# First attention layer of an audio tower: scores over 32-row tiles, in two parts around the transposes of x_q

## The chip, the cores and the metric

The kernel runs on one core of a Trainium2 chip. The metric is the device time of one execution in microseconds (us). Before the change three executions took 4547.76, 4551.70 and 4551.86 us, a median of 4551.7 us. The core has a matrix engine (TensorE, PE in the profile, with its weight loads listed apart as PEld), a vector engine (DVE), a scalar engine (ACT), a general engine (POOL) and a queue for transfers (SP). Each runs its own list of instructions strictly in the order in which it was written, and they meet only at semaphores.

## The reference

The input is 64 sequences of 375 frames of 256 features. What is computed is this; the change touches the fourth line alone.

```
x  = conv(x, width 2, stride 2) + mean of the two frames      # 64 x 188 x 256
h  = layernorm(x) * gamma + beta
q, k, v = layernorm(h) @ qkv_proj.T + qkv_bias                # 16 heads of 16
attn = softmax(SCALE * einsum('bld,bmd->blm', q, k))          # b: token and head; l, m: the 64 sequences
h  = h + einsum('blm,bmd->bld', attn, v) @ out_proj.T + out_bias
xq = fp4_quant_dequant(layernorm(h))                          # blocks of 16
h  = h + fp4_quant_dequant(silu(xq @ wgate) * (xq @ wup)) @ wdown
h  = h + linear_attention(layernorm(h))                       # second layer, 16 heads of 64
h  = h + 0.5 * ffn(layernorm(h))                              # second layer
```

The attention of the first layer goes over the first axis of its input, so for each of the 188 tokens and each of the 16 heads there is a 64 x 64 table of scores with an inner size of 16.

## The kernel before, in words

`layer0` handles two tokens at a time: a tile has 128 rows, 64 sequences of one token and 64 of the next, and there are 94 tiles (`TILES`). The work is a software pipeline written out by hand. Each engine has a function `slot(t, par)`, and slot `t` holds the convolution of tile `t`, the attention of tile `t-1` and `t-2`, and the feed-forward part of the tiles `t-3` and `t-4`. Slots 0 to 5 and the last ones are written out; the ones between are a loop over pairs of slots. `exists(t, lag)` leaves out what has no tile. The order of the calls in each `slot` is the order on that engine, and nothing else decides it. `bank_free` and `wait` are waits on counts of finished steps.

On TensorE the slot runs: `conv`, `v_product` (L340), `xq_transpose` (L331, tile `xq`), `scores` (L369), then `gate(t, 0)`, `att_transpose`, `hq_transpose`, `up(t, 0)`, `outproj`, `gate(t, 1)`, `up(t, 1)`, `down`, `ln1_transpose`, `p_transpose`, `qk_product` and `pv_product` (L464). The products written as `product3` (L1093 to L1095) are three matmuls over high and low parts. A plain fp32 matmul shows as two weight loads and two matmuls in the records.

The scores need one block per head. Heads have 16 features, and a matmul takes 64 rows (4 heads) at a time. So `k_copy` on ACT (L571) writes k four times into `kblk`, each copy with all heads but one of each four masked to zero by the per-row scale `rowmask` and the masked bias `kb_masked`:

```python
for j in range(4):
    act.activation(kblk[:, c, :, j, :], src, ACT.Identity, bias=kb_masked[:, c, j:j + 1],
                   scale=rowmask[:, j:j + 1]).then_inc(S["qk_copied"], 1)
```

It does so for the two halves of the features (`KC` is 2), 8 activations in all, and `q_copy` (L562) behind it adds 2. `scores` waits until all ten are counted (`QK`). It then issues 8 matmuls: for each `c` one for each of the four quadrants of the array, 64 rows by 64 columns, with 256 moving columns (4 heads of 64 keys).

Three chains meet here. TensorE transposes `xq` into bank `tp`; ACT copies it out (`xq_copy`, `xqT_hi`), DVE makes the low part (`xq_low`, L857, `xqT_lo`), and `gate(t, 0)` waits for that (`xqT_split`). DVE's `score_max` (L779, `rowmax`) waits for `scores_done`. And ACT gets to `k_copy` only behind `xq_magnitude` (`binade_x`), which waits for DVE.

Of the kernel before, what the change touches and what calls it, by code (L numbers as in the profile page):

```python
# [156 lines left out]
def layer0(nc, x, conv_w, conv_b, tok_g, tok_b, qkv_w, q_b, k_b, v_b, out_w, out_b, gate_w, up_w, down_w,  # L157
           h2_dram, ident, eps, exponent, w1, w1_loaded, wq, wk, wv, wo):
    with ExitStack() as ctx:
# [3 lines left out]
        def sem(name):  # L163
# [10 lines left out]
        vb_wide = sb("vb_wide", [128, KC, 128])  # L174
        eighths, rowmask, kb_masked = sb("eighths", [128, 8]), sb("rowmask", [128, 4]), sb("kb_masked", [128, KC, 4])

# [8 lines left out]
        qT = sb("qT", [128, KC, 128])  # L185
        kblk = sb("kblk", [128, KC, 2, 4, 64])
        vblk = [sb(f"vblk{i}", [128, PAIRS, 2, VW]) for i in range(2)]
# [44 lines left out]
            "ln1_ready", "ln1_transposed", "ln1T_copied", "qk_done", "v_done", "qk_copied", "vblk_ready",  # L232
            "scores_done", "shift_step", "probs_ready", "p_transposed", "PT_copied", "pv_done", "att_step",
            "att_transposed", "attT_copied", "outproj_done", "h1_step", "h1b_ready", "ln2_ready", "xq_step", "xabs_ready", "xq_ready",
            "xq_transposed", "xqT_copied", "xqT_split", "gate_done", "up_done", "tanh_done", "hh_step", "hqa_step", "hv_ready", "habs_ready", "hqb_step",
            "hq_ready", "hq_transposed", "hqT_copied", "hqT_split", "down_done", "h2_ready", "h2_stored0", "h2_stored1")}

        QK, YS, H1S, ST1, HH, SHIFT, ATT = KC + 4 * KC, 3, 3, 2, 4, 2, 2
        XM = SCALE_OPS + 1
# [39 lines left out]
        with nc.Block() as block:  # L279
# [47 lines left out]
            def _(pe):  # L327
# [30 lines left out]

                def scores(t):
                    if isinstance(t, int) and t == 1:  # L360
                        pe.wait_ge(wfold, 6 + 2 * KC)
                    wait(pe, "qk_copied", t, QK)
                    wait(pe, "att_step", t - 1, ATT)
                    pe.sem_inc(S["scores_seen"], 1)
                    for c in range(KC):
                        for r in range(2):
                            for n in range(2):
                                p = slice(64 * r, 64 * r + 64)
                                last = pe.matmul(sc[64 * n:64 * n + 64, r, 256 * c:256 * (c + 1)],  # L369
                                                 qT[p, c, 64 * n:64 * n + 64], kblk[p, c, n, :, :], start=True, stop=True)  # L370
                    last.then_inc(S["scores_done"], 1)

# [96 lines left out]
                def slot(t, par):  # L469
                    if exists(t, 0):  # L470
                        conv(t, par)
                    if exists(t, 1):
                        v_product(t)
                    if exists(t, 3):
                        xq_transpose(t)
                    if exists(t, 1):
                        scores(t)
                    if isinstance(t, int) and t == 2:
                        weight_jobs("gate")
                    if isinstance(t, int) and t == 4:  # L480
                        down_jobs()
                    if exists(t, 3):
                        gate(t, 0)
                    if exists(t, 2):
                        att_transpose(t)
                    if exists(t, 4):
                        hq_transpose(t)
                    if exists(t, 3):
                        up(t, 0)
                    if exists(t, 2):  # L490
                        outproj(t)
                    if isinstance(t, int) and t == 2:
                        weight_jobs("up")
                    if exists(t, 3):
                        gate(t, 1)
                        up(t, 1)
                    if exists(t, 4):
                        down(t)
                    if exists(t, 0):
                        ln1_transpose(t)  # L500
                    if exists(t, 1):
                        p_transpose(t)
                    if exists(t, 0):
                        qk_product(t)
                    if exists(t, 1):
                        pv_product(t, 1 - par)
# [46 lines left out]
            def _(act):  # L553
# [11 lines left out]
                def k_copy(t):  # L565
                    wait(act, "qk_done", t + 1)
                    wait(act, "scores_done", t)
                    for c in range(KC):
                        src = gu[:, 0, 256 + 128 * c:256 + 128 * (c + 1)].rearrange("p (n k) -> p n k", n=2)
                        for j in range(4):  # L570
                            act.activation(kblk[:, c, :, j, :], src, ACT.Identity, bias=kb_masked[:, c, j:j + 1],  # L571
# [142 lines left out]
                def weights(t):  # L714
                    if t == 0:
# [3 lines left out]
                        act.wait_ge(wsmall, 16 * 6)  # L719
                        act.wait_ge(wfold, 5 + 2 * KC)  # L720

# [27 lines left out]
            def _(dve):  # L749
# [198 lines left out]
                def weights(t):  # L948
                    if t == 0:
# [20 lines left out]
                        for c in range(KC):  # L970
                            dve.tensor_copy(vb_wide[:, c, :], vb_col[:, c:c + 1].broadcast_to([128, 128])).then_inc(wfold, 1)
                        dve.tensor_tensor(rowmask[:], eighths[:, 0:4], eighths[:, 4:8], ALU.add).then_inc(wfold, 1)
                        dve.wait_ge(wfold, 5 + KC)
                        for c in range(KC):
                            dve.tensor_scalar(kb_masked[:, c, :], rowmask[:], kb_col[:, c:c + 1], None, ALU.mult)\
# [27 lines left out]
            def _(pool):  # L1003
# [58 lines left out]
                def weights(t):  # L1062
# [18 lines left out]
                    if t == 1:  # L1081
                        weight_values("gate")
                        pool.wait_ge(wfold, 6 + 2 * KC)
                    if t == 3:
# [789 lines left out]
```

## Time and profile before

| | us |
|---|---|
| median of 3 executions | 4551.7 |
| profiled execution, its own time | 4539.33 |
| span of the profiled execution | 4536.7 |
| PE busy, weight loads busy | 4354.9 (96%), 3972.3 (88%) |
| DVE busy | 3317.8 (73%) |
| ACT busy | 2712.1 (60%) |
| POOL busy | 2100.0 (46%) |

The span runs from the first to the last instruction. TensorE's granted clock is 0.983 of full speed in the mean. The first layer takes about the first 1640 us and the second the rest. The shares are means over both; in the first layer DVE is far busier than in the second. Busy time of matmuls is modelled and overlaps, so for TensorE the distance from the start of one step's weight loads to the start of the next step's is the safer reading, and it is the one used below.

### The profile page before, as it was taken

The numbers are of one execution on the slowest core, as the hardware profiler recorded it, in microseconds if no ns is written. First come the engines' busy times: TensorE is split into PE (matmuls) and PEld (weight loads), VectorE is DVE, ScalarE is ACT, GpSimd is POOL, SyncE is SP. The second block draws the span as 40 slices with busy tenths as digits, with TensorE's granted clock in tenths as the row PEclk, the third lists the DMA queues.
The fourth block names the chain that finished last, engine by engine and source line by source line (L and its number), as shares of the span: only waits on it lengthen the run. The fifth ranks groups of instructions, "written<-read, shape, count | busy, mean of one in ns | idle before, by whom it ended". The sixth has DMA issues, their size and how long they took to land.

```text
span 4536.7 us, 121660 instructions
## 1 busy us (share of the span) xinstructions
PE 4354.9 (96%) x43948; PEld 3972.3 (88%) x43948; DVE 3317.8 (73%) x7106; ACT 2712.1 (60%) x5662; POOL 2100.0 (46%) x2682
## 2 busy tenths in 40 slices
PE   5999999999999958999999999999999999999997
PEld 4889999999899848899999999999999999989996
DVE  6999999999999845666666666666666666666665
ACT  4777777777777734555555555555555555545553
POOL 4566666666666522433433443343343344334333
PEclk8999999999999979999999999999999999999998
DMA  2100000000000010000000000000000000000000
GB/s 71 43 24 24 24 24 24 23 22 24 24 24 24 21 45 5 5 15 8 9 15 9 9 12 12 9 11 13 9 9 15 9 9 14 10 9 8 15 5 11
DMA packets 64982, 79.21 MB, mean 17 GB/s; under 512 B 8800, under 2 KB 51168, under 8 KB 64480
## 3 DMA queue, kind: packets, MB, share of 16 engines
q1 hardware_dynamic: 64608, 74.07, 5.6%
q8 instruction: 254, 4.16, 0.4%
q14 instruction: 120, 0.98, 0.1%
HBM read 49.40 MB, written 24.64 MB: 16 GB/s over the span
## 4 chain that ended last, share of the span: by engine, by line
PE 56%; DVE 3%; issue 2%; ACT 1%; POOL 1%; ACTq 0%; DVEq 0%; POOLq 0%
PE bA L1093 11%; PE bA L1095 9%; PE bA L1094 9%; PE bS L1398 4%; PE bO L1420 3%; PE bA L1484 3%; PE bB L1093 2%; PE bB L1094 2%; PE bB L1384 2%; PE bB L1095 2%; PE bB L1383 2%; PE bA L1485 2%; PE bT L1436 2%; PE bO L1424 1%; PE bO L1429 1%
## 5 line engine op out<-in xcount | busy, mean ns | idle before, releaser
L1820 POOL TENSOR_TENSOR sqs_lo<-sq,sqs_hi 128x768 fp32r<-128x768 f32 x256 | 480.6, 1878 | 673.9 <-ACT sqs_hi L1535 670.1
L1634 DVE TENSOR_TENSOR qk_lo<-bA,qk_hi 128x384 fp32r<-128x384 f32 x512 | 284.3, 556 | 517.1 <-ACT qk_hi L1535 516.8
L1554 ACT ACTIVATE phi<-bB 128x768 f32<-128x768 f32 x256 | 207.4, 810 | 662.5 <-PE bB L1384 662.5
L1778 POOL TENSOR_TENSOR yT_lo<-tanh_y,yT_hi 128x384 fp32r<-128x384 f32 x256 | 259.3, 1013 | 545.0 <-ACT yT_hi L1535 545.0
L1535 ACT ACTIVATE qk_hi<-bA 128x384 fp32r<-128x384 f32 x512 | 251.9, 492 | 195.2 <-PE bA L1095 188.0
L1644 DVE TENSOR_TENSOR aT<-bS,mask 128x1024 f32<-128x1024 f32 x256 | 311.0, 1215 | 1.3 <-PE bS L1403 1.3
L1544 ACT ACTIVATE sq<-bA 128x384 f32<-128x384 f32 x512 | 250.2, 489 | 62.1 <-DVE qk_lo L1634 61.3
L571 ACT ACTIVATE kblk<-gu,kb_masked,rowmask 128x128 f32<-128x128 f32 x752 | 271.7, 465 | 5.1 <-PE gu L452 5.0
L1093 PE MATMUL bA<-fc_lo,yT_hi 128*128 128x256 f32 x768 | 230.7, 300 | 13.1 <-POOL yT_lo L1778 6.4
L1093 PE MATMUL bA<-wv_lo,xT_hi 128*128 128x256 f32 x768 | 230.0, 300 | 5.9 <-ACT sq L1544 1.3
L1093 PE MATMUL bA<-wo_lo,attT_hi 128*128 128x256 f32 x768 | 226.3, 295 | 9.8 <-ACT sq L1544 2.1
L1484 PE MATMUL bA<-hT_lo,fc_w 128*128 128x384 f32 x512 | 213.3, 417 | 18.1 <-DVE xT_lo L1634 11.2
L1152 POOL TENSOR_TENSOR rstd<-moments,eps 128x3 f32<-128x3 f32 x96 | 20.8, 217 | 446.8 <-DVE moments L1162 446.8
L640 ACT ACTIVATE ln<-h,nbias,rstd 128x256 f32<-128x256 f32 x188 | 112.9, 601 | 190.5 <-POOL nbias L1011 190.5
L1398 PE MATMUL bS<-phi 64*64 64x192 f32 x4096 | 225.5, 335 | 0.0
L1420 PE MATMUL bO<-V,aT 128*64 128x65 f32 x4096 | 219.3, 228 | 0.0
L1095 PE MATMUL bA<-fc_hi,yT_hi 128*128 128x256 f32 x768 | 217.6, 283 | 0.0
L1094 PE MATMUL bA<-fc_hi,yT_lo 128*128 128x256 f32 x768 | 217.5, 283 | 0.0
L1094 PE MATMUL bA<-wv_hi,xT_lo 128*128 128x256 f32 x768 | 216.4, 282 | 0.0
L1095 PE MATMUL bA<-wv_hi,xT_hi 128*128 128x256 f32 x768 | 216.3, 282 | 0.0
L1535 ACT ACTIVATE sqs_hi<-sq 128x768 fp32r<-128x768 f32 x256 | 214.5, 838 | 1.2
L1095 PE MATMUL bA<-wo_hi,attT_hi 128*128 128x256 f32 x768 | 214.4, 279 | 0.0
(269 smaller groups left out, 16222.6 us busy)
## 6 DMA issues: line engine op xcount, KB each, us to landing
xT<-in_x SPq DMA_DIRECT2D x94, 256.0 KB, 2.6
h_scratch<-h SPq DMA_DIRECT2D x188, 64.0 KB, 1.9
hx<-h_scratch SPq DMA_DIRECT2D x32, 256.0 KB, 2.7
out<-res SPq DMA_DIRECT2D x32, 256.0 KB, 2.2
hx<-h_scratch SPq DMA_DIRECT2D x64, 64.0 KB, 2.4
out<-res SPq DMA_DIRECT2D x64, 60.0 KB, 1.8
q<-in_fc_q SPq DMA_DIRECT2D x2, 1024.0 KB, 7.7
wq_sb<-in_wq SPq DMA_DIRECT2D x1, 1024.0 KB, 5.0
```

Source lines behind the costliest of these rows:

```text
L571: act.activation(kblk[:, c, :, j, :], src, ACT.Identity, bias=kb_masked[:, c, j:j + 1], scale=rowmask[:, j:j + 1]).then_inc(S["qk_copied"], 1)
L1093: pe.matmul(out, lhs[0], rhs[1], start=start, stop=False)
L1094: pe.matmul(out, lhs[1], rhs[0], start=False, stop=False)
L1095: return pe.matmul(out, lhs[0], rhs[0], start=False, stop=stop)
L1398: pe.matmul(SC[o:o + 64, h, q], phi[b][p, 1, k], phi[b][p, 0, q], start=True, stop=True)
L1420: pe.matmul(O[o:o + 64, dst(i)], aT[b][:, h, HEADS[i] + o:HEADS[i] + o + 64], V[:, i, v], start=True, stop=True)
L1484: pe.matmul(A[:, k, 0:NT], w, hT[1][:, k, :], start=True, stop=False)
L1535: act.activation(dst, src, ACT.Copy).then_inc(S[done], 1)
L1634: dve.tensor_tensor(dst, src, hi.bitcast(fp32), ALU.subtract).then_inc(S[done], 1)
L1644: dve.tensor_tensor(aT[b][:], SC[:, :, 0:ST], mask[:].unsqueeze(1).broadcast_to([128, 2, ST]), ALU.mult)\
L1778: pool.tensor_tensor(yT[1][:, f % RING, :], tanh_y[f % 2][:], yT[0][:, f % RING, :].bitcast(fp32), ALU.subtract).then_inc(S["y_lo"], 1)
L1820: pool.tensor_tensor(sqs[1][:], sq[:], sqs[0][:].bitcast(fp32), ALU.subtract).then_inc(S["sq_lo"], 1)
```

## The change

`scores` becomes `scores(t, m)` with `m` 0 and 1. Part `m` takes rows 32m to 32m+31 of each 64, which is 2 heads, against `kblk` with two masked copies instead of four, and writes 128 columns. So there are 8 matmuls of 32 rows and 128 moving columns in a part and 16 in all, in the place of 8 of 64 rows and 256 columns. Part 0 stands ahead of `xq_transpose`, part 1 behind it. Part 0 takes over the waits for k, q and the attention before it; part 1 waits for part 0 to be finished (`scores_half`), and the last matmul of part 1 raises `scores_done`. `k_copy` has 4 activations instead of 8. The mask for two copies is folded once more at the start, by one small DVE instruction.

```diff
-        kblk = sb("kblk", [128, KC, 2, 4, 64])
+        kblk = sb("kblk", [128, KC, 2, 2, 64])
...
-        QK, YS, H1S, ST1, HH, SHIFT, ATT = KC + 4 * KC, 3, 3, 2, 4, 2, 2
+        QK, YS, H1S, ST1, HH, SHIFT, ATT = KC + 2 * KC, 3, 3, 2, 4, 2, 2
...
-                def scores(t):
-                    if isinstance(t, int) and t == 1:
-                        pe.wait_ge(wfold, 6 + 2 * KC)
-                    wait(pe, "qk_copied", t, QK)
-                    wait(pe, "att_step", t - 1, ATT)
+                def scores(t, m):
+                    if m == 0:
+                        if isinstance(t, int) and t == 1:
+                            pe.wait_ge(wfold, 7 + 2 * KC)
+                        wait(pe, "qk_copied", t, QK)
+                        wait(pe, "att_step", t - 1, ATT)
+                    else:
+                        wait(pe, "scores_half", t)
                     pe.sem_inc(S["scores_seen"], 1)
                     for c in range(KC):
                         for r in range(2):
                             for n in range(2):
-                                p = slice(64 * r, 64 * r + 64)
-                                last = pe.matmul(sc[64 * n:64 * n + 64, r, 256 * c:256 * (c + 1)],
-                                                 qT[p, c, 64 * n:64 * n + 64], kblk[p, c, n, :, :], start=True, stop=True)
-                    last.then_inc(S["scores_done"], 1)
+                                p = slice(64 * r + 32 * m, 64 * r + 32 * m + 32)
+                                o = 256 * c + 128 * m
+                                last = pe.matmul(sc[64 * n:64 * n + 64, r, o:o + 128], qT[p, c, 64 * n:64 * n + 64],
+                                                 kblk[p, c, n, :, :], start=True, stop=True)
+                    last.then_inc(S["scores_half" if m == 0 else "scores_done"], 1)
...
                     if exists(t, 1):
                         v_product(t)
+                    if exists(t, 1):
+                        scores(t, 0)
                     if exists(t, 3):
                         xq_transpose(t)
                     if exists(t, 1):
-                        scores(t)
+                        scores(t, 1)
...
-                        for j in range(4):
+                        for j in range(2):
...
-                        dve.tensor_tensor(rowmask[:], eighths[:, 0:4], eighths[:, 4:8], ALU.add).then_inc(wfold, 1)
+                        dve.tensor_tensor(fourths[:], eighths[:, 0:4], eighths[:, 4:8], ALU.add).then_inc(wfold, 1)
                         dve.wait_ge(wfold, 5 + KC)
+                        dve.tensor_tensor(rowmask[:], fourths[:, 0:2], fourths[:, 2:4], ALU.add).then_inc(wfold, 1)
+                        dve.wait_ge(wfold, 6 + KC)
```

TensorE's list in a slot of the loop, from the value product to the first matmul of the gate, was this before (`gu`, `sc` and `bank` are PSUM tiles; REGISTER_ALU and ISA rows carry waits and counts):

```order
L340 MATMUL gu<-v_sb,ln1T 64x128 [waits ln1T_copied,hh_step]
L340 MATMUL gu<-v_sb,ln1T 64x128 x7
L63 REGISTER_ALU [waits ln1T_copied]
L331 MATMUL bank<-ident,xq 128x128 [waits xq_ready]
L331 MATMUL bank<-ident,xq 128x128
L63 REGISTER_ALU
L63 ISA [waits qk_copied]
L369 MATMUL sc<-kblk,qT 64x256 [waits att_step]
L369 MATMUL sc<-kblk,qT 64x256 x7
L253 ISA
L1093 MATMUL gu<-gate_lo,xqT_hi 128x352 [waits xqT_split,qk_copied]
```

The same place of the same engine now:

```order
L340 MATMUL gu<-v_sb,ln1T 64x128 [waits ln1T_copied,hh_step]
L340 MATMUL gu<-v_sb,ln1T 64x128 x7
L63 REGISTER_ALU
L63 ISA [waits qk_copied]
L373 MATMUL sc<-kblk,qT 64x128 [waits att_step]
L373 MATMUL sc<-kblk,qT 64x128 x7
L63 REGISTER_ALU [waits ln1T_copied]
L331 MATMUL bank<-ident,xq 128x128 [waits xq_ready]
L331 MATMUL bank<-ident,xq 128x128
L373 MATMUL sc<-kblk,qT 64x128 [waits scores_half]
L373 MATMUL sc<-kblk,qT 64x128 x7
```

Eight score matmuls, with the wait for k and q, moved ahead of the transposes of `xq`; eight stand behind them with a wait of their own.

On ACT, the stretch from `binade_x` to the copy of the transposed `xq`, before:

```order
L558 ACTIVATE binade_x<-ln 128x256
L571 ACTIVATE kblk<-gu,kb_masked,rowmask 128x2x64 x8
L562 ACTIVATE qT<-gu,qb_col 128x128 x2
L555 ACTIVATE xqT_hi<-bank 128x256
L555 ACTIVATE vblk<-gu 64x8x16 x4
```

and now:

```order
L564 ACTIVATE binade_x<-ln 128x256
L577 ACTIVATE kblk<-gu,kb_masked,rowmask 128x2x64 x4
L568 ACTIVATE qT<-gu,qb_col 128x128 x2
L561 ACTIVATE xqT_hi<-bank 128x256
L561 ACTIVATE vblk<-gu 64x8x16 x4
```

Four of the eight copies are gone; the rest stands in the same order.

## Rows read from the trace of the kernel before

**Rows 1.** Busy time by stretch: columns PE, PEld, DVE, ACT, POOL, clock, DMA, GB/s.

```profile
200.00:800.00 600.00, 597.23 (x5789) 540.42 (x5786) 547.95 (x1203) 462.82 (x1104) 364.29 (x693) 1.00 0.09 24
```

**Rows 2.** Timeline of TensorE's weight loads, one slot: start, us, engine, line, tile, count.

```profile
905.51 1.01 PEld L464 LDWEIGHTS sc<-vblk,PT_sb 128*64 128x64 f32 x32
906.57 0.19 PEld L1093 LDWEIGHTS bank<-conv_lo,xT_hi 128*128 128x128 f32 x1
...
908.18 0.90 PEld L340 LDWEIGHTS gu<-v_sb,ln1T 128*64 128x64 f32 x16
909.25 0.20 PEld L331 LDWEIGHTS bank<-ident,xq 128*128 128x128 f32 x2 [0.17 <-issue]
909.74 0.67 PEld L369 LDWEIGHTS sc<-kblk,qT 64*64 64x64 f32 x16 [0.29 <-issue]
910.80 0.19 PEld L1093 LDWEIGHTS gu<-gate_lo,xqT_hi 128*128 128x128 f32 x1 [0.39 <-issue]
...
922.97 0.19 PEld L1093 LDWEIGHTS bank<-conv_lo,xT_hi 128*128 128x128 f32 x1
```

**Rows 3.** Waits in 600 to 1200 us, longest first: us in total, times, longest.

```profile
DVE ln L127 <- ACT binade_x L558: 17.4, 36, 0.5
PEld gu L1093 <- issue: 14.3, 36, 0.4
PEld sc L369 <- issue: 10.0, 36, 0.3
PEld bank L331 <- issue: 6.2, 36, 0.2
DVE rowmax L779 <- PE sc L369: 5.1, 28, 0.2
```

**Rows 4.** Timeline of ACT, same slot, and the copies of k two slots later.

```profile
906.13 2.89 ACT L571 ACTIVATE kblk<-gu,kb_masked,rowmask 128x128 f32<-128x128 f32 x8
908.88 0.66 ACT L562 ACTIVATE qT<-gu,qb_col 128x128 f32<-128x128 f32 x2
909.81 0.38 ACT L555 ACTIVATE xqT_hi<-bank 128x256 fp32r<-128x256 f32 x1 [0.27 <-PE bank L331]
...
938.94 1.49 ACT L571 ACTIVATE kblk<-gu,kb_masked,rowmask 128x128 f32<-128x128 f32 x4
```

**Rows 5.** Timeline of DVE, same slot.

```profile
909.88 0.43 DVE L752 BATCH_NORM_STATS2 stats<-y 128x6 f32<-128x256 f32 x1
910.23 0.42 DVE L857 TENSOR_TENSOR xqT_lo<-bank,xqT_hi 128x256 fp32r<-128x256 f32 x1
...
910.92 1.23 DVE L779 TENSOR_REDUCE rowmax<-sc 128x16 f32<-128x1024 f32 x1 [0.17 <-PE sc L369]
```

**Rows 6.** Timeline of slots 3 and 4, where other waits set the order.

```profile
77.48 0.20 PEld L331 LDWEIGHTS bank<-ident,xq 128*128 128x128 f32 x2 [0.17 <-issue]
77.85 0.64 PEld L369 LDWEIGHTS sc<-kblk,qT 64*64 64x64 f32 x16 [0.17 <-issue]
...
82.55 0.41 DVE L857 TENSOR_TENSOR xqT_lo<-bank,xqT_hi 128x256 fp32r<-128x256 f32 x1
...
83.07 0.19 PEld L1093 LDWEIGHTS gu<-gate_lo,xqT_hi 128*128 128x128 f32 x1 [4.58 <-issue]
...
99.34 0.67 PEld L369 LDWEIGHTS sc<-kblk,qT 64*64 64x64 f32 x16 [0.31 <-issue]
...
100.39 0.31 PEld L546 LDWEIGHTS pt<-ident,draw 128*128 128x128 f32 x3 [0.39 <-issue]
...
107.27 0.51 DVE L794 SCALAR_TENSOR_TENSOR hh<-tanh_g,gu 128x352 f32<-128x352 f32 x1
...
107.83 0.19 PEld L1093 LDWEIGHTS gu<-gate_lo,xqT_hi 128*128 128x128 f32 x1 [0.58 <-DVE hh L794]
```

**Rows 7.** Weight loads of the q and k products, whole array, 128 moving columns.

```profile
903.52 0.97 PEld L452 LDWEIGHTS gu<-ln1T,q_sb 128*128 128x128 f32 x8
904.42 0.97 PEld L452 LDWEIGHTS gu<-ln1T,k_sb 128*128 128x128 f32 x8
```

More of the change, by code:

```diff
@@ L174, in layer0 @@
         vb_wide = sb("vb_wide", [128, KC, 128])
-        eighths, rowmask, kb_masked = sb("eighths", [128, 8]), sb("rowmask", [128, 4]), sb("kb_masked", [128, KC, 4])
+        eighths, fourths, rowmask, kb_masked = sb("eighths", [128, 8]), sb("fourths", [128, 4]), sb("rowmask", [128, 2]), sb("kb_masked", [128, KC, 2])
         conv_w0 = tuple(sb(f"conv_{p}", [128, 2 * KC, DM], fp32r) for p in ("hi", "lo"))
@@ L232, in layer0 @@
             "ln1_ready", "ln1_transposed", "ln1T_copied", "qk_done", "v_done", "qk_copied", "vblk_ready",
-            "scores_done", "shift_step", "probs_ready", "p_transposed", "PT_copied", "pv_done", "att_step",
+            "scores_half", "scores_done", "shift_step", "probs_ready", "p_transposed", "PT_copied", "pv_done", "att_step",
             "att_transposed", "attT_copied", "outproj_done", "h1_step", "h1b_ready", "ln2_ready", "xq_step", "xabs_ready", "xq_ready",
@@ L719, in weights @@
                         act.wait_ge(wsmall, 16 * 6)
-                        act.wait_ge(wfold, 5 + 2 * KC)
+                        act.wait_ge(wfold, 6 + 2 * KC)
                 def split(h):
@@ L1082, in weights @@
                         weight_values("gate")
-                        pool.wait_ge(wfold, 6 + 2 * KC)
+                        pool.wait_ge(wfold, 7 + 2 * KC)
                     if t == 3:
```

## The prediction

> **What bounds the kernel now.** I read the stretches first. In the first layer TensorE is busy 597 of 600 us and DVE 548 of 600 [rows 1], so two engines are nearly full, and a busy share can't say which of them sets the pace. The second layer is not touched, so everything below is the first layer's slot, repeated 94 times.
>
> Next come the weight loads of one slot. The convolution starts at 906.57 and the next one at 922.97, a slot of 16.40 us [rows 2]. The list of waits for 600 to 1200 us, some 37 slots, has only three entries for TensorE's loads, and all three lie between the value product and the gate: 0.17 us before the transposes of x_q, 0.28 before the scores, 0.40 before the gate [rows 3]. From the gate's start at 910.80 to the next value product TensorE goes through its list without a wait. So a delay of the gate's start is a delay of the whole slot, and the slot can shrink only between 908.18 and 910.80.
>
> What ends in that stretch: the transposes start at 909.25, and ACT's copy of them at 909.81, with ACT idle for 0.27 us before and released by TensorE [rows 4]. DVE's low part starts at 910.23, which is 0.04 us after ACT's copy ends (909.81 + 0.38 = 910.19), and ends at 910.65 [rows 5]. DVE is also just done with its statistics then, so both reach that point together. A wait of TensorE on DVE costs 0.11 us where x_q's low part was late (82.96 to 83.07) and 0.05 us on hh (107.78 to 107.83) [rows 6], so this chain lets the gate start at 910.70 to 910.76. The other chain is the scores: q's copy ends at 909.54, the scores start at 909.74, and they hold the array for 1.05 us, because in slot 4, where other transposes with no wait on DVE followed them, these came 1.05 us later as well (99.34 to 100.39) [rows 2, 4, 6]. That gives 910.79. The two chains that release the gate end within 0.1 us of each other: transposes, ACT, DVE on one side, k and q copies and scores on the other.
>
> **The change part by part.** *The copies of k.* Eight activations take 2.89 us and four take 1.49 [rows 4], so q's copy ends 1.40 us earlier, at 908.14, before the value product has left the array at 909.25. The wait of the scores on q goes. What it was worth: the transposes and scores start 0.49 us apart now and 0.37 where q was early [rows 2, 6], so 0.12 us, and that only on the scores' chain. What is late next is the x_q chain, which has under 0.1 us of slack. The shorter copies alone are worth 0.03 to 0.10 us a slot.
>
> *The scores.* Before, all of them lay behind the transposes, under the time that ACT and DVE need for x_q's parts. Now part 0 lies ahead, where nothing covers it. The two parts take the place of a block of 1.05 us. Each part has again 16 weight loads and 16 matmuls in the records, with half the columns. The trace has no tile of 32 rows, so I bound the price of one part from both sides. Below: the 32 matmuls of the PV product, 34 columns, take 1.06 us from their start to the convolution [rows 2], 0.033 each, so 16 take 0.53. Above: the value product has the same 16 matmuls with the same 128 columns in only two tiles and takes 1.07 us [rows 2]. Nearest is the scores' own block in four tiles: 0.17 us of it I take as the empty stretch at a change of step (the idle time before the transposes), and half of the remaining 0.88 is 0.44, so 0.61; I add 0.02 for the extra waits and take 0.63.
>
> A load's time follows its columns and not its rows, says the Trainium skill ("TensorE: Matmul & The Clock Gate", LDWEIGHTS), so the 16 additional loads are as dear as the old ones though they carry half the rows; by its figure an estimate is 16 x 64 / 1.2 = 0.85 us where they hide behind nothing, which would put a part near the upper bound. The same page (Measured speedup vs the span model) gives four row tiles of 32 a speedup of 3.07, not 4; by that the 0.44 would be 0.57 and the time some 12 us longer than my sum. No run here shows a 32-row tile yet.
>
> *The new slot.* Value product 908.18, part 0 at 909.25, x_q's transposes at 909.25 + 0.63 = 909.88. Part 1 follows 0.37 later, at 910.25, and leaves the array at 910.88; its wait for part 0 is over by then, since the transposes stand between. The transposes' chain keeps its lengths: 0.56 us to ACT's copy (909.25 to 909.81), 0.38, 0.04, 0.42 on DVE, and 0.08 (the middle of 0.05 and 0.11) to the gate: 909.88 + 1.48 = 911.36. This is 0.48 behind the end of part 1, so part 1 is hidden and part 0 is not. The gate moves from 910.80 to 911.36, +0.56 us a slot. By the bounds of a part: 0.53 with 0.05 gives +0.43, 1.07 with 0.11 gives +1.03.
>
> *DVE.* It waits for x_q's high part until 910.86 in place of being just in time, then has moments and rowmax. The scores are done by then, so its wait of 0.17 us for them goes [rows 5]. Its own work plus waits filled 16.40 us with that 0.17, so it needs 16.23 and has 0.7 us to spare in a slot of 16.96. ACT and POOL have more. Neither takes the pace from TensorE. Of what lies behind the later steps on ACT, the four copies of v follow x_q's copy and move by the same 0.63; the gate's tanh found ACT idle before, and the gate moves by 0.56, so 0.07 us of it is eaten there without reaching TensorE.
>
> *Counts.* Both x_q's transposes and scores exist in slots 3 to 94. In slot 3 the gate waits 4.58 us for DVE anyway [rows 6], which hides the shift, and in slot 4 the jobs for the down weights stand before the gate. 90 slots are left: 90 x 0.56 = 50.4 us. Slots 1 and 2 have no transposes of x_q; there each gains up to 1.40 us by shorter copies if q is waited for. I take 2 us for both. One more small DVE instruction at the start is under 0.1 us. The profiled execution took 4539.3 us with a span of 4536.7; its sum is 4539.3 + 50.4 - 2 = 4587.7. It was 12.4 us faster than the median of the runs, so against that the forecast is 4600 us, 1.1% slower.
>
> **The rivals.**
>
> *Faster, the copies decide.* If DVE and ACT set the pace, the loop is DVE's scaled ln, ACT's binade_x, copies of k and q, scores, rowmax, and it has 0.17 us of waiting on the scores. With 1.40 us out of it the slot falls to 16.23: 90 x 0.17 + 2 = 17 us, 4534 us. For it speaks that DVE really waits for the scores in 28 of some 37 slots [rows 3]. It needs the gate to start no later than 910.63, while part 0 lies ahead of the transposes; it decides only if part 0 costs nothing, that is if x_q's chain had over 0.6 us of slack. Against it stands ACT's idle time released by the transposes, and 0.04 us between ACT and DVE.
>
> *No change.* TensorE's stretch from gate to convolution could hold stops that the view doesn't list, of about half a microsecond, in which the lost time is made good. Then the slot stays at 16.40 and the time at 4550. Against it: every one of the steps there starts on the heels of the one before, and the list names no wait.
>
> *The tiles of 32 rows overlap less.* At the value product's rate a part takes 1.07 us, the transposes start at 910.32, part 1 ends at 911.76 and the x_q chain at 911.80: +1.00 a slot, 4551.7 + 90 - 2 = 4640 us. With no overlap at all, at the 0.1125 us per matmul of the q and k products (0.90 / 8) [rows 7], a part takes 16 x 0.1125 + 0.17 = 1.97, the two with the transposes between fill 909.25 to 913.56, +2.76 a slot and 4798 us. For both speaks only that no such tile is in the trace; against them, that the 64 x 64 tiles reach 0.055 us for 256 columns (0.88 / 16), half of what a whole-array matmul needs for 128, which takes four at once.
>
> **How the numbers follow.** The forecast, with its bounds, has 0.79 (own range 4588 to 4625); the 1.07 us part 0.07; no overlap 0.02; no change 0.05; faster 0.07. A measurement of this kernel tells 0.2%, about 9 us, from no change. The range of 8 in 10 goes from 4580, a little under the lower bound of the part, to 4642, which takes in the value product's rate; it leaves out 0.14. Faster by over 0.2%: 0.07. Within 0.2%: 0.05. Slower: 0.88.
>
> **What would show each step.** In the profile of the changed kernel the loads of the scores should stand in two groups of 16, the first right behind the value product, about 0.63 us before x_q's transposes; q's copy should end over 1 us before it is wanted; the copies of k should take 1.49 us; DVE's wait on the scores should be gone, and a new one of about 0.6 us, on ACT's x_q copy, should stand before xqT_lo, in nearly every slot; the gate should wait about half a microsecond for DVE with the array empty; and the slot should be 16.96 us. A slot below 16.5 would refute the claim that TensorE's order sets the pace. A part of about 1.0 us would mean that the tiles of 32 rows overlap less. If the second layer differs at all, the comparison is disturbed.

## The result and the profile after

The changed kernel takes 4592.7 us in the median of 4 runs (4588.0 to 4597.1) against 4550.9 of 4 runs before: 1.0093 times as long, 95% interval 1.0075 to 1.0110, so 34 to 50 us more. The profiled execution has a span of 4595.4 us and took 4597.1.

The busy time by stretch, columns as in [rows 1]. TensorE falls from 597 to 582 us of 600 and DVE from 548 to 527: no engine has more to do in a stretch than before, and both wait more.

```profile
200.00:800.00 600.00, 582.20 (x6164) 531.57 (x6162) 527.37 (x1165) 394.65 (x919) 350.94 (x667) 1.00 0.09 24
```

The weight loads of one slot, as in [rows 2]:

```profile
918.00 0.90 PEld L340 LDWEIGHTS gu<-v_sb,ln1T 128*64 128x64 f32 x16
919.08 0.42 PEld L373 LDWEIGHTS sc<-kblk,qT 32*64 32x64 f32 x16 [0.17 <-issue]
919.67 0.20 PEld L331 LDWEIGHTS bank<-ident,xq 128*128 128x128 f32 x2 [0.17 <-issue]
920.04 0.42 PEld L373 LDWEIGHTS sc<-kblk,qT 32*64 32x64 f32 x16 [0.17 <-issue]
...
921.19 0.19 PEld L1101 LDWEIGHTS gu<-gate_lo,xqT_hi 128*128 128x128 f32 x1 [0.72 <-issue]
...
934.97 0.90 PEld L340 LDWEIGHTS gu<-v_sb,ln1T 128*64 128x64 f32 x16
```

Part 0 takes 0.59 us (919.08 to 919.67), part 1 follows the transposes by 0.37, and the gate, which came 2.62 us behind the value product in [rows 2], comes 3.19 behind it. One value product to the next is 16.97 us. In the mean of 78 slots it is 17.00, and of 80 slots before 16.41 (the start of the first value product behind 160 us and behind 1480 us, over the number of slots between).

DVE of the same slot, as in [rows 5]. It sits idle for 0.58 us before x_q's low part, released by ACT, and goes to rowmax without a wait. A wait of 0.43 us stands before DVE's product with the result of `up` (`hh`).

```profile
920.65 0.42 DVE L863 TENSOR_TENSOR xqT_lo<-bank,xqT_hi 128x256 fp32r<-128x256 f32 x1 [0.58 <-ACT xqT_hi L561]
...
924.38 0.52 DVE L807 TENSOR_TENSOR hh<-hh,gu 128x352 f32<-128x352 f32 x1 [0.43 <-PE gu L1103]
```

ACT, as in [rows 4]: the copies of k take half as long, and the engine then waits 2.35 us for TensorE.

```profile
915.89 1.49 ACT L577 ACTIVATE kblk<-gu,kb_masked,rowmask 128x128 f32<-128x128 f32 x4
917.25 0.63 ACT L568 ACTIVATE qT<-gu,qb_col 128x128 f32<-128x128 f32 x2
920.23 0.38 ACT L561 ACTIVATE xqT_hi<-bank 128x256 fp32r<-128x256 f32 x1 [2.35 <-PE bank L331]
```

The waits in 600 to 1200 us, answering [rows 3]. The wait of rowmax on the scores is gone from the list, and the gate's idle time has grown from 0.40 to 0.72 us a slot (25.2 / 35).

```profile
PEld gu L1101 <- issue: 25.2, 35, 0.7
DVE xqT_lo L863 <- ACT xqT_hi L561: 19.2, 35, 0.6
PE gu L1101 <- DVE xqT_lo L863: 17.8, 35, 0.5
DVE hh L807 <- PE gu L1103: 14.1, 36, 0.4
```

The last of these is not new. The same list of the kernel before has it further down, in about half of the slots:

```profile
DVE hh L801 <- PE gu L1095: 3.6, 19, 0.2
```

The second layer begins where the rows of one of its products begin. The row of the kernel before, from the view of that tile; the pair behind the durations is the first and the last start:

```profile
L1384 PEld LDWEIGHTS bB<-sqs_hi,norm x512: 187/188/334, 1680.1 to 4447.0; 128*128 128x128 f32 x171
```

The same row of the changed kernel:

```profile
L1392 PEld LDWEIGHTS bB<-sqs_hi,norm x512: 187/188/334, 1727.6 to 4504.5; 128*128 128x128 f32 x171
```

The first layer lost 47.5 us. The second, whose source is untouched, took 2776.9 us from the first of these to the last in place of 2766.9. Of the 58.7 us between the two profiled spans 10 are thus lost in a layer that the change doesn't touch; "Why the second layer moves" comes back to them.

### The profile page after: what moved, and what is told of

It is laid out like the page before. It is cut to its first block, busy times and chain, and to the rows that moved or that the text cites. A ratio compares the mean times of both kernels' runs of the same rounds, so it can differ in the third digit from the quotient of the medians.

```text
span 4595.4 us, 124387 instructions
## 1 busy us (share of the span) xinstructions
PE 4376.5 (95%) x45452; PEld 4005.1 (87%) x45452; DVE 3318.7 (72%) x7107; ACT 2574.7 (56%) x5286; POOL 2098.6 (46%) x2682
## 4 chain that ended last, share of the span: by engine, by line
PE 56%; DVE 3%; issue 2%; ACT 1%; POOL 1%; ACTq 0%; DVEq 0%; POOLq 0%
PE bA L1101 11%; PE bA L1103 9%; PE bA L1102 9%; PE bS L1406 4%; PE bO L1428 3%; PE bA L1492 3%; PE bB L1101 2%; PE bB L1103 2%; PE bB L1102 2%; PE bB L1391 2%; PE bB L1392 2%; PE bA L1493 2%; PE bT L1444 1%; PE bO L1437 1%; PE bO L1432 1%
## 5 line engine op out<-in xcount | busy, mean ns | idle before, releaser
L1102 PE MATMUL bA<-wo_hi,attT_lo 128*128 128x256 f32 x768 | 215.0, 280 | 0.0
```

Source lines behind the costliest of these rows:

```text
L1102: pe.matmul(out, lhs[1], rhs[0], start=False, stop=False)
```

## The experiments

Eleven kernels ran, on chips where before took 4543, 4550 and 4542 us in the median of its runs in that series. Each ratio is to before in its own series. "Slot" is the mean over 73 to 81 slots, read as above; "second layer" is the distance between the two starts just shown.

| kernel | ratio to before, interval | slot, us | second layer starts at, takes |
|---|---|---|---|
| before | 1 | 16.41 | 1680.1, 2766.9 |
| changed | 1.0093 [1.0075, 1.0110] | 17.00 | 1727.6, 2776.9 |
| tall tiles, half ahead | 1.0150 [1.0134, 1.0165] | 16.98 | 1730.0, 2790.3 |
| both parts behind | 1.0029 [1.0019, 1.0039] | 16.68 | 1700.6, 2763.2 |
| copies alone | 0.9981 [0.9972, 0.9990] | 16.39 | 1674.4, 2766.9 |
| whole block ahead | 1.0301 [1.0285, 1.0316] | 17.92 | 1815.8, 2768.6 |
| part 0 left out | 1.0038 [1.0024, 1.0052] | 16.41 | 1680.2, 2790.0 |
| x_q first, block tall | 0.9996 [0.9987, 1.0005] | 16.41 | 1679.6, 2764.8 |
| x_q first, split wait | 1.0041 [1.0027, 1.0054] | 16.37 | 1674.3, 2798.1 |
| x_q, part 0, v, part 1 | 0.9980 [0.9971, 0.9989] | 16.36 | 1680.5, 2767.1 |
| split wait, TensorE shifted | 0.9998 [0.9988, 1.0007] | 16.37 | 1677.6, 2774.4 |
| split wait, ACT shifted | 1.0041 [1.0025, 1.0056] | 16.37 | 1675.8, 2790.1 |
| changed, TensorE shifted | 1.0083 [1.0070, 1.0097] | 17.00 | 1728.9, 2761.4 |

**Is it the place or the tile?** The kernel before keeps its 64-row tiles and four copies, and only half of its block moves ahead. Part 0 is here the first half of the features (`c` 0) and waits for the first five of the ten copies, which ACT writes first; part 1 is the other half. TensorE's order changes so:

```diff
+                    if exists(t, 1):
+                        scores(t, 0)
                     if exists(t, 3):
                         xq_transpose(t)
                     if exists(t, 1):
-                        scores(t)
+                        scores(t, 1)
```

> The kernel before with its 64-row tiles and all four copies of k, but the scores in two parts by feature half: the four tall matmuls of c = 0 ahead of x_q's transposes, those of c = 1 behind them. ACT writes the four copies of c = 0 and q's first half first, so that part 0 is not late. Theory (place: whatever TensorE issues between the value product and x_q's transposes lengthens the slot by its own time): a part takes about 0.6 us, as in the changed kernel, and the slot is 16.95 to 17.00 us, some +0.57 over before, 4595 to 4605 us in all. Rival (the 32-row tiles, their doubled instruction count or the two copies are the cost): the slot stays near 16.4 us and the time near 4552.

TensorE's weight loads of one slot of it:

```profile
918.49 0.90 PEld L340 LDWEIGHTS gu<-v_sb,ln1T 128*64 128x64 f32 x16
919.57 0.21 PEld L372 LDWEIGHTS sc<-kblk,qT 64*64 64x64 f32 x8 [0.17 <-issue]
920.16 0.20 PEld L331 LDWEIGHTS bank<-ident,xq 128*128 128x128 f32 x2 [0.39 <-issue]
920.53 0.21 PEld L372 LDWEIGHTS sc<-kblk,qT 64*64 64x64 f32 x8 [0.17 <-issue]
921.67 0.19 PEld L1099 LDWEIGHTS gu<-gate_lo,xqT_hi 128*128 128x128 f32 x1 [0.94 <-issue]
```

Four tall matmuls with 256 columns take the same 0.59 us as eight short ones with 128, everything behind them falls on the same places to 0.01 us, and the slot is 16.98. So neither the 32-row tiles nor twice the matmuls nor the number of copies makes the loss; the place does. (In total this kernel is slower than expected, 4613 us in a series where before was 4543; the second layer accounts for 23 us of that.)

**Undo the place alone.** The changed kernel with both parts behind the transposes:

```diff
-                    if exists(t, 1):
-                        scores(t, 0)
                     if exists(t, 3):
                         xq_transpose(t)
                     if exists(t, 1):
+                        scores(t, 0)
                         scores(t, 1)
```

> The changed kernel with both parts behind x_q's transposes: 32-row tiles, two copies, 16 matmuls, only the place undone. Theory (place): the parts are under the x_q chain again. Part 0 starts 0.37 us after the transposes, 0.59 us each plus about 0.1 for the wait of part 1 on part 0, so the gate could start 1.65 us behind the transposes in place of 1.55: slot 16.40 to 16.55, time 4548 to 4563 us. Rival (32-row tiles and more instructions cost the 0.56 us a slot): slot 16.9, time near 4593. Rival (the shorter copies set the pace once the place is right): slot 16.23, time 4535.

Its weight loads of one slot:

```profile
920.17 0.20 PEld L331 LDWEIGHTS bank<-ident,xq 128*128 128x128 f32 x2 [0.17 <-issue]
920.54 0.42 PEld L373 LDWEIGHTS sc<-kblk,qT 32*64 32x64 f32 x16 [0.17 <-issue]
921.36 0.45 PEld L373 LDWEIGHTS sc<-kblk,qT 32*64 32x64 f32 x16 [0.39 <-issue]
921.98 0.19 PEld L1100 LDWEIGHTS gu<-gate_lo,xqT_hi 128*128 128x128 f32 x1 [0.17 <-issue]
```

More than half of the loss goes (first layer +20.5 us in place of +47.5), but the slot of 16.68 is above the 16.40 to 16.55 that I expected. The parts are 0.82 us apart, not 0.59: part 1 waits until part 0 is finished, which costs 0.23 us where nothing stands between them. With the last stop before the gate the pair takes 1.44 us in place of the block's 1.05. So in this order, with the value product ahead of the transposes, the halves are not free in either place: side by side they pay the wait, and apart one of them lies where nothing covers it. (An order in which both are covered comes below.)

**Leave the exposed part out.** Part 0's matmuls are not issued, so half of the scores are not computed:

```diff
-                        scores(t, 0)
+                        pe.sem_inc(S["scores_half"], 1)
```

> The changed kernel with part 0's matmuls left out (half of the scores are not computed; its count is raised by hand and the waits for q and k stand before part 1). Theory (what stands ahead of x_q's transposes is exposed, what stands behind is hidden): the gate starts where the x_q chain puts it, 1.48 us behind the transposes, the slot falls from 16.97 to 16.35 to 16.40 us, the whole of the loss is gone: -52 to -58 us against the changed kernel, some 4535 to 4541 where before is 4543. Rival (the second wait and the doubled number of short matmuls cost something by themselves, wherever they stand): the slot stays above 16.6 us.

Its weight loads from the transposes to the gate:

```profile
924.50 0.20 PEld L331 LDWEIGHTS bank<-ident,xq 128*128 128x128 f32 x2 [0.17 <-issue]
...
926.01 0.19 PEld L1103 LDWEIGHTS gu<-gate_lo,xqT_hi 128*128 128x128 f32 x1 [0.72 <-issue]
```

The slot is 16.41 again, 0.01 over the range that I gave, and the second layer starts at 1680.2, as before. The gate stands 1.51 us behind the transposes and idles the same 0.72 us as in the changed kernel, so part 1 is hidden fully and part 0 is the whole loss. The total, 1.0038, doesn't show this, because the second layer took 23 us more.

**More of it ahead.** The kernel before with its whole block ahead of the transposes:

```diff
                     if exists(t, 1):
+                        scores(t)
+                    if exists(t, 3):
                         xq_transpose(t)
-                    if exists(t, 1):
-                        scores(t)
```

> The kernel before with its whole scores block ahead of x_q's transposes; nothing else changed, four copies. Theory (place): q is ready for TensorE at 909.74 on the scale of the slot shown, the block holds the array 1.05 us, the transposes start at 910.79 and the gate 1.48 us later at 912.27, +1.47 us a slot over before: slot 17.87 us, about +132 us, 4684 us. Rival (other engines set the pace and TensorE's order is worth little): under +60 us.

Its weight loads, value product to gate:

```profile
927.56 0.90 PEld L340 LDWEIGHTS gu<-v_sb,ln1T 128*64 128x64 f32 x16
929.10 0.67 PEld L369 LDWEIGHTS sc<-kblk,qT 64*64 64x64 f32 x16 [0.64 <-issue]
930.15 0.20 PEld L331 LDWEIGHTS bank<-ident,xq 128*128 128x128 f32 x2 [0.39 <-issue]
931.67 0.19 PEld L1093 LDWEIGHTS gu<-gate_lo,xqT_hi 128*128 128x128 f32 x1 [1.31 <-issue]
```

17.92 us a slot against the 17.87 expected, and 135 us in all (4678.0 against 4542.8) where 132 were expected. The delay of the transposes, by 0.47 us of waiting for q and 1.05 of matmuls, arrives whole in the slot.

**The copies alone.** In the kernel before, two of the four copies are left out, so half of `kblk` keeps zeros and half of the scores are not computed from k; the count `QK` falls with them, and the tall matmuls stay as they were:

```diff
-                        for j in range(4):
+                        for j in range(2):
```

> The kernel before, with two of the four masked copies of k left out (half of kblk keeps zeros, so half of the scores are not computed from k); the 64-row matmuls and their place stay. Theory: q is ready 1.40 us earlier, the scores start 0.12 us earlier, and then the x_q chain ends last, so the slot falls by 0.03 to 0.10 us, 3 to 11 us in all: 4541 to 4549. Rival (the copies set the pace): slot 16.23 us, 4534 us or less. DVE's wait on the scores of 0.17 us should shrink to about 0.05 to 0.10 us, not to nothing, by the theory.

The list of waits before had DVE waiting for the scores in 28 of some 37 slots [rows 3]. Here, in the same stretch, it has no such row, but these:

```profile
PEld gu L1095 <- issue: 18.8, 36, 0.6
DVE hh L801 <- PE gu L1097: 9.2, 36, 0.3
PEld sc L369 <- issue: 6.1, 36, 0.2
```

The total fell by 0.19% (0.10 to 0.28), the slot by 0.02 to 0.03 us. The 0.11 us that the scores waited for q (10.0 us in [rows 3], 6.1 here, over 36 slots) went; the gate then waits for the x_q chain, as expected. The wait of DVE on the scores is gone altogether, and the expectation of 0.05 to 0.10 us was wrong there, but DVE now waits 0.26 us a slot for the product with `up`, in every slot, where before it was 0.19 us in 19 of them.

**Can the changed form be made to pay?** Two orders of the kernel before first. Ahead of the value product stands nothing but the convolution, in the same tile shape:

```diff
+                    if exists(t, 3):
+                        xq_transpose(t)
                     if exists(t, 1):
                         v_product(t)
-                    if exists(t, 3):
-                        xq_transpose(t)
-                    if exists(t, 1):
                         scores(t)
```

> The kernel before with x_q's transposes moved ahead of the value product, scores untouched. Theory: the x_q chain gets 1.3 us of slack, but the scores still wait for q until 909.74 and hold the array 1.05 us, so the gate starts at 910.79 as before and DVE waits for the scores as before: slot 16.40, 4540 to 4546 where before is 4543. Rival (x_q's chain alone had set the pace): slot 16.23 us, 4526 us.

Slot 16.41 and no difference in all, as expected. The waits in 600 to 1200 us have rowmax behind the scores as before, 0.2 us a slot:

```profile
DVE rowmax L778 <- PE sc L369: 7.3, 36, 0.2
```

But the slack that I had counted on for x_q's chain is not there. The transposes of this slot start at 907.42; of the 1.3 us that they gain, ACT's copy keeps 0.4, because it stands behind q's copy in ACT's list, and DVE's low part keeps nothing:

```profile
908.82 0.43 ACT L554 ACTIVATE xqT_hi<-bank 128x256 fp32r<-128x256 f32 x1
...
909.68 0.41 DVE L856 TENSOR_TENSOR xqT_lo<-bank,xqT_hi 128x256 fp32r<-128x256 f32 x1
```

The copy ends at 909.25, and DVE takes the low part 0.43 us later, right behind its own statistics; the gate follows 0.56 us after that (910.24), as before (0.57). So in the kernel before it is DVE's own list as much as the transposes that sets when the low part comes.

Next the same order, with the copies of the first feature half and its q written first, and the first half of the block waiting for those five only:

```diff
-                    wait(pe, "qk_copied", t, QK)
+                    wait_step(pe, "qk_copied", t - 1, QK, 5)
...
                     for c in range(KC):
+                        if c == 1:
+                            wait(pe, "qk_copied", t, QK)
+                            pe.sem_inc(S["scores_seen"], 1)
```

> As the kernel with x_q's transposes ahead of the value product, and ACT writes the four copies and q of the first feature half before those of the second; the tall scores stay one block whose first half waits for the first five of the ten copies only. Theory: both chains are off the path; TensorE could start the gate at 910.5, so DVE's own work sets the slot: 16.23 to 16.30 us, -9 to -16 us, 4527 to 4534 where before is 4543, and DVE waits for nobody but binade_x. Rival (TensorE's list with its fixed stops is as long as the slot anyway): 16.40 us, 4543 us.

The slot is 16.37, 0.05 us shorter, and not the 16.23 to 16.30 expected. What is late is named by the waits in 600 to 1200 us:

```profile
DVE hh L803 <- PE gu L1097: 14.2, 36, 0.4
PE gu L1095 <- DVE xqT_lo L859: 8.6, 36, 0.3
```

The gate waits for x_q's low part on DVE, and 3 us later DVE waits 0.39 us for the `up` product, which TensorE could not start earlier because of that gate. This is a loop from DVE over TensorE back to DVE. Once around, in this kernel:

```profile
906.30 0.41 DVE L859 TENSOR_TENSOR xqT_lo<-bank,xqT_hi 128x256 fp32r<-128x256 f32 x1
906.82 0.19 PEld L1095 LDWEIGHTS gu<-gate_lo,xqT_hi 128*128 128x128 f32 x1 [0.68 <-issue]
910.02 0.52 DVE L803 TENSOR_TENSOR hh<-hh,gu 128x352 f32<-128x352 f32 x1 [0.36 <-PE gu L1097]
...
922.65 0.41 DVE L859 TENSOR_TENSOR xqT_lo<-bank,xqT_hi 128x256 fp32r<-128x256 f32 x1
```

From the low part to the gate are 0.52 us, from the gate over `up` to DVE's product 3.20, and from there through DVE's list to the next low part 12.63: 16.35. The kernel before goes the same way round. Its low part is at 910.23 and its gate at 910.80 [rows 2, 5], and DVE's product follows at

```profile
913.99 0.52 DVE L801 TENSOR_TENSOR hh<-hh,gu 128x352 f32<-128x352 f32 x1
```

which makes 0.57, 3.19 and, of a slot of 16.40, 12.64 for the rest. The only part that the edits here could shorten is the first: the gate stands 0.57 us behind the low part in the kernel before, where the scores hold it up, and 0.52 to 0.54 in the kernels where they don't. That is why taking off waits around the scores brings 0.05 us and no more. In the changed kernel the three parts are 0.54, 3.19 and 13.24, and the last has the 0.58 us in it that DVE idles before the low part.

The version that is faster than both kernels takes the changed form and sets x_q's transposes first, then part 0, the value product and part 1:

```diff
-                    if exists(t, 1):
-                        v_product(t)
-                    if exists(t, 1):
-                        scores(t, 0)
                     if exists(t, 3):
                         xq_transpose(t)
                     if exists(t, 1):
+                        scores(t, 0)
+                        v_product(t)
                         scores(t, 1)
```

> The changed kernel in another order: x_q's transposes, part 0, value product, part 1; two copies and 32-row tiles as changed. Theory: nothing stands ahead of the transposes any more but the convolution, the value product covers the wait of part 1 on part 0. TensorE needs 0.37 + 0.59 + 1.07 + 0.62 = 2.65 us from the transposes to the gate, which now start 0.2 us earlier as no change of tile shape stands before them; that gives 16.23 to 16.35 us a slot, 4527 to 4538 where before is 4543 and the changed kernel 4585. Rival (32-row tiles lose by themselves): slot above 16.6 us, 4560 us or more.

Its weight loads from the convolution's last to the gate's first:

```profile
920.57 0.19 PEld L1101 LDWEIGHTS bank<-conv_hi,xT_hi 128*128 128x128 f32 x1
920.71 0.24 PEld L331 LDWEIGHTS bank<-ident,xq 128*128 128x128 f32 x2
921.12 0.42 PEld L373 LDWEIGHTS sc<-kblk,qT 32*64 32x64 f32 x16 [0.17 <-issue]
921.71 0.90 PEld L340 LDWEIGHTS gu<-v_sb,ln1T 128*64 128x64 f32 x16 [0.17 <-issue]
922.78 0.42 PEld L373 LDWEIGHTS sc<-kblk,qT 32*64 32x64 f32 x16 [0.17 <-issue]
923.47 0.19 PEld L1099 LDWEIGHTS gu<-gate_lo,xqT_hi 128*128 128x128 f32 x1 [0.26 <-issue]
```

4540.6 us where before is 4550.1: 0.20% faster (0.11 to 0.29). The transposes follow the convolution's last load by 0.14 us, where the value product followed it by 0.33; part 0 and the value product lie under the time of x_q's chain; and the value product covers the wait of part 1. The slot of 16.36 is 0.01 over the range that I gave; it is the length of the loop over `up`, and DVE waits for that product in 31 slots here (5.8 us in all). TensorE's own list isn't what holds the slot: part 1 could leave the array at 923.37 (922.78 + 0.59), 0.10 us before the gate starts. The slot accounts for some 5 us of the 9.5 by which the medians differ. In the profiled execution even these are gone at the end of the first layer (the second starts at 1680.5, before at 1680.1), so the rest is not explained. Against the changed kernel it is 1.1% better with every instruction kept.

**Why the second layer moves.** The list of waits of the second layer (1700 to 4400 us) for the kernel with the split wait has this row:

```profile
PEld bB L1095 <- issue: 18.5, 5, 3.8
```

and that of the kernel before this one:

```profile
PEld bB L1093 <- issue: 2.7, 5, 0.6
```

Two of the long stops, in the timeline:

```profile
2973.38 0.29 PEld L1095 LDWEIGHTS bB<-qk_lo,omega_hi 128*128 128x128 f32 x1 [3.76 <-issue]
...
3327.98 0.29 PEld L1095 LDWEIGHTS bB<-qk_lo,omega_hi 128*128 128x128 f32 x1 [3.48 <-issue]
```

They come at the same matmul, 355 us apart. The stops alone are 18.5 of the 31 us by which this second layer is longer than before's. Most of the rest is the clock: while TensorE stands still the granted clock falls from 1.00 to 0.50, from 2.4 to 1.2 GHz, and it is back only 6.8 us later (columns as in [rows 1]).

```profile
2972.20:2979.00 6.80, 5.62 (x18) 5.62 (x19) 0.00 (x0) 0.91 (x2) 3.38 (x2) 0.50 0.01 2
```

It does so at all five stops, with TensorE busy for 28.2 us at the lower level. Half of that, 14 us, is my estimate of what it costs, and with the 18.5 it comes near the 31. Sixteen counting instructions between the layers, first in TensorE's list, then in ACT's in place of it, then in TensorE's list of the changed kernel:

```diff
                 slots(pe, slot, weights)
+                for _ in range(16):
+                    pe.sem_inc(S["scores_seen"], 1)
```

> The kernel with x_q's transposes first and the split wait, with 16 counting instructions added to TensorE's list between the two layers; they cost under 1 us and only shift the second layer's code. The first layer's slot stays 16.37 us. Theory (the second layer of that kernel lost 31 us against before because its code lies elsewhere, with a stop of 3.5 to 3.8 us once in each pass of its loop): the stops change in size or go, and with them 10 to 31 us; without them 4535 to 4545 where before is 4550, on the scale of the last series. Rival (the second layer is slower because of what the first left behind): 4566 again.

> The same, with the 16 counting instructions in ACT's list and not in TensorE's. By the theory that it is the place of TensorE's own code that counts, the stops of the second layer stay (4566 on the scale of the last series); if the place of any engine's code counts, they may change.

> The changed kernel with the same 16 counting instructions on TensorE between the layers. The slot of the first layer stays 16.97 to 17.00 us. Its second layer took 10 us longer than before's in the profiled execution; by the theory of code placement this may go away or grow, so 4575 to 4610 where before is 4550, with the first layer unmoved.

With TensorE's code shifted the stops are half as long, the clock is low for 3.4 us at three of them, and the second layer is 24 us shorter (2774.4). With ACT's shifted the stops stay, though this layer, too, is 8 us shorter than without a shift (2790.1). The row of the list of waits with TensorE's code shifted:

```profile
PEld bB L1097 <- issue: 9.2, 5, 2.3
```

and with ACT's:

```profile
PEld bB L1097 <- issue: 19.1, 5, 4.0
```

The changed kernel has none of these long stops (2.6 us in 5). Its second layer has four waits of 2.2 us for DVE's `xT_lo` where before's longest was 0.6, and these are gone with the shift, which takes the second layer from 2776.9 to 2761.4 us; the first layer stays: the second starts at 1728.9, and the slot is 17.00. Its ratio of 1.0083 is that of the change with a second layer 5.5 us shorter than before's.

## Why the prediction was right

The forecast was 4600 us, 48 more; measured were 42 more (34 to 50), inside the forecast's own range, and 47.5 in the first layer of the profiled execution. By its steps:

*What bounds.* "A delay of the gate's start is a delay of the whole slot": part 0 left out, half ahead, and all ahead gave 0, +0.57 and +1.51 us a slot, with the transposes 0, 0.60 and 1.52 us later. Right. That the two chains before the gate end within 0.1 us of each other also held: shortening the scores' chain by the copies brought 0.02 us, transposing x_q earlier brought nothing, and only both together brought 0.05. What this part left open is why the slot could not be shorter: it looked for that on TensorE alone, and the loop over DVE decides it.

*The copies.* 1.49 us and q early by over 1 us, as said; taken to be worth 0.03 to 0.10 us a slot alone, and measured 0.02 to 0.03, with some 3 us more outside the loop of slots.

*A part.* Taken at 0.63 us, measured 0.59. The bound of 0.53 from the PV product and of 1.07 from the value product held, and the scores' own block in four tiles was the right neighbour: the tiles of 32 rows overlap as the tall ones do. The additional loads hide. In 600 to 1200 us a load takes 131 ns with 32 rows and 132 ns with 64. This is as the Trainium skill has it ("TensorE: Matmul & The Clock Gate", LDWEIGHTS), by which a load's time goes by its columns and not by its rows. The same page (Measured speedup vs the span model) gives four row tiles of 32 a speedup of 3.07 and not 4, which the prediction weighed as 0.13 us more for a part. A part of 0.59 leaves no room for that; but the page's four tiles lie one below the other, and the four of a part are two by two, so its figure itself is not tested here.

*The chain and the slot.* 1.48 us from the transposes to the gate, measured 1.52 (919.67 to 921.19): 0.56, 0.38, 0.04 and 0.42 as said, and 0.12 for TensorE's wait on DVE where I took 0.08. Part and chain erred by 0.04 us each and against each other, so that the slot of 16.97 shown is within 0.01 us of the 16.96 forecast is luck. The predicted signs were all there: the wait on ACT of half a microsecond before x_q's low part, no wait of rowmax, the gate idle with the array empty.

*The counts.* 90 slots at 0.58 are 52 us; the first layer lost 47.5, so the start and the end of the layer gave back 4 to 5 us where I had 2. The second layer added 10 us that no step had; the prediction had named such a difference as a disturbance of the comparison. The medians differ by 42 us and the profiled executions by 58, because the one before was 12 us under the median of its runs and the one after 4 us over. That the total came within 7 us of the forecast is thus closer than its parts were.

*The rivals.* "The tiles overlap less" and "the copies decide" fell by the rows above. The second was priced too high as well: it gave DVE's own work as 16.23 us a slot, found by taking off the one wait of 0.17. In every kernel in which that wait went, the wait on `up` grew in its place, and none came under 16.36. The step left out was the loop from x_q's low part over gate and `up` to DVE's product, and its wait, 0.2 us in 19 slots, already stood in the list of waits of the kernel before.

## What to carry to other kernels

Where TensorE runs a fixed list, look for the instruction whose result goes out over other engines and comes back to release the next big product, and put nothing ahead of it that could stand behind it: ahead, work costs its own time (0.59 us for half a block here); behind, it costs nothing as long as it fits into the time that the result is away. Before splitting a block to fill such a gap, check that the gap isn't already filled; here the block lay under the chain whole. And taking off one wait rarely frees all of it: price the next-longest loop, not the wait, and follow it across engines, also over a wait that shows in half of the slots only.

## What the runs showed that I had not expected

The untouched second layer took between 2761 and 2798 us in thirteen kernels, 1.3% apart, which is more than most of the edits are worth. In the slowest, TensorE stops for 3.5 to 3.8 us at one matmul about every 355 us with nothing that the profile names, and the granted clock halves for 6.8 us around the end of each stop. Sixteen instructions more in TensorE's list ahead of the loop halve these stops, the same sixteen in ACT's don't. So it is TensorE's list that decides. Whether by the place of its code or by the moment at which it enters the loop, these runs do not tell apart. For verdicts under 1% the slot of the changed layer is therefore the measure, and totals only between kernels whose second layers agree.

A part that waits for another of the same size to be finished starts 0.82 us behind it where nothing stands between, 0.23 us later than the other's own 0.59. With the transposes' 0.37 us between them no such wait shows.
